# Two residual 64x64 products per batch: the first four units of eight batches in 32x64 TensorE tiles with half-partition stores, the other twelve in 32x128 tiles

## What is computed

```
x = x + einsum('bct,bcd->bdt', x, w0[subjects])      # 8 matrices of 64x64
x = x + einsum('bct,bcd->bdt', x, w1[conditions])    # 200 matrices of 64x64
```

## Time and profile before

| | us |
|---|---|
| median of 3 runs | 92.75 (92.61 to 92.92) |
| the profiled execution | 92.78 |
| its span, first to last instruction | 91.0 |
| outside the span | 1.8 |
| TensorE busy | 78.5 (86%) |
| DVE busy | 61.8 (68%) |
| ACT busy | 58.6 (64%) |
| POOL busy | 23.4 (26%) |
| TensorE's granted clock, mean | 0.989 |

### The profile page before, as it was taken

How to read it: one execution, slowest core, us unless ns; L and a number is a source line. 1 busy time by engine, 2 the same in 40 slices (tenths; PEclk the granted TensorE clock), 3 DMA queues, 4 the chain that set the end, 5 groups by cost and what they waited for, 6 DMA issues and landing times.

```text
span 91.0 us, 2427 instructions
## 1 busy us (share of the span) xinstructions
PE 78.5 (86%) x890; PEld 44.7 (49%) x890; DVE 61.8 (68%) x127; ACT 58.6 (64%) x117; POOL 23.4 (26%) x119
## 2 busy tenths in 40 slices
PE   0499939994999999999999999999999999999200
PEld 0389929983554544364454445445454544444000
DVE  1087008995288888796887878788777888778700
ACT  2899806886276767585777667677666777577500
POOL 3400029999999959300000000000000000000000
PEclk9999999999999999999999999999999999999995
DMA  0999989999999999999999999999999999999993
GB/s 9 334 411 421 461 342 427 412 412 407 411 411 402 412 400 414 409 421 420 418 418 414 423 420 418 416 418 421 423 407 423 418 418 421 421 414 376 414 420 140
DMA packets 9181, 35.93 MB, mean 395 GB/s; under 512 B 721, under 2 KB 850, under 8 KB 9042
## 3 DMA queue, kind: packets, MB, share of 16 engines
q1 hardware_dynamic: 4512, 16.78, 46.3%
q10 hardware_dynamic: 4514, 16.91, 45.8%
q0 software_dynamic: 144, 2.10, 5.4%
HBM read 19.01 MB, written 16.78 MB: 393 GB/s over the span
## 4 chain that ended last, share of the span: by engine, by line
PE 70%; DMA 13%; DVE 9%; issue 1%; DVEq 1%; ACTq 0%; POOLq 0%
PE psum L219 62%; DMA w_rows<-in_L_cond_weights_dram,cond 10%; DVE w L238 7%; PE psum L200 7%; DMA subjects<-in_itok_B_dram 2%; DVEq L69 1%; DVE xy L260 1%; PE psum L180 1%; DVE m_diag L252 1%; ACTq L318 0%; DVE w_rows L313 0%; POOLq L149 0%; DVEq L244 0%
## 5 line engine op out<-in xcount | busy, mean ns | idle before, releaser
L219 PE MATMUL psum<-xy,m_diag 64*128 64x512 f32 x256 | 57.1, 596 | 0.5 <-DVE m_diag L252 0.5
L260 DVE COPY xy<-psum 64x512 f32<-64x512 f32 x64 | 43.7, 683 | 13.2 <-PE psum L219 12.2
L260 ACT COPY xy<-psum 64x512 f32<-64x512 f32 x64 | 37.2, 581 | 19.8 <-PE psum L219 19.0
L219 PEld LDWEIGHTS psum<-xy,m_diag 64*128 64x128 f32 x256 | 24.8, 187 | 27.1 <-issue 25.7
L157 POOL COPY w0b<-w0t 64x64 f32 x112 | 21.6, 235 | 11.0 <-DMA w_rows<-in_L_cond_weights_dram,cond 8.5
L200 PEld LDWEIGHTS psum<-w,w0b 64*32 64x32 f32 x512 | 5.6, 105 | 6.4 <-issue 3.8
L238 ACT COPY w<-psum 64x256 f32<-64x256 f32 x16 | 5.8, 364 | 4.1 <-PE psum L180 3.1
L180 PE MATMUL psum<-ident,w_rows 128*64 128x128 f32 x64 | 7.2, 274 | 1.4 <-DVE w_rows L313 1.4
L252 DVE TENSOR_SCALAR m_diag<-psum,mask 128x256 f32<-128x256 f32 (+1 forms) x18 | 7.3, 449 | 1.1 <-PE psum L200 0.9
L326 ACT COPY w<-w_rows 128x256 f32<-128x256 f32 x18 | 7.3, 405 | 0.9 <-DMA w_rows<-in_L_cond_weights_dram 0.3
L180 PEld LDWEIGHTS psum<-ident,w_rows 128*64 128x64 f32 x64 | 7.0, 152 | 1.6 <-DVE w_rows L313 1.6
(11 more groups left out here) (8 smaller groups left out, 2.3 us busy)
## 6 DMA issues: line engine op xcount, KB each, us to landing
xy<-in_x_dram SPq DMA_DIRECT2D x15, 1024.0 KB, 19.0
out_dram<-xy ACTq DMA_DIRECT2D x15, 1024.0 KB, 11.0
xy<-in_x_dram SPq DMA_DIRECT2D x2, 512.0 KB, 5.9
out_dram<-xy ACTq DMA_DIRECT2D x2, 512.0 KB, 4.3
w_rows<-in_L_cond_weights_dram ACTq DMA_DIRECT2D x1, 128.0 KB, 2.6
cond<-in_itok_B_dram SPq DMA_DIRECT2D x1, 0.5 KB, 2.4
subjects<-in_itok_B_dram ACTq DMA_DIRECT2D x1, 0.5 KB
w_rows<-in_L_cond_weights_dram,cond POOLq DMA_INDIRECT x1, 9.5
```

Of the source, the lines that this page charges most:

```text
L219: last = nc.tensor.matmul(psum[:, 2 * (s % Y_RING) + h, :], m_diag[rows, odd, v % M_RING, j, :], xy[rows, s, j * T:(j + 1) * T], start=j = ...
L260: copy(xy[rows, s, i * T:(i + 1) * T], psum[HALVES[i], 2 * (s % Y_RING) + h, :]).then_inc(done, 1)
```

## The change

The first four units (`SINGLE`) are stored in SBUF as before, in slots. Their stationary operand is now one batch's M alone, `m_single`, with no zeros, in tiles of 32 rows by 64 columns (`apply_single`). What leaves PSUM has one batch's 64 output channels on 64 partitions, four batches side by side, so a unit is stored by two DMAs, each from 64 partitions, in descriptors of one row (2 KB).

The other twelve units lie with four rows of x (8 KB) in a partition and 16 partitions for a batch (`J = 4`), are loaded by one DMA of 1 MB in descriptors of 8 KB, and are multiplied in four tiles of 32 rows by 128 columns with `m_diag` (two batches on the diagonal), four steps `j` for each half of a unit, the second half one step behind the first. Their products are made for two batches at a time with 128 moving columns, of which the mask keeps half. Their stores are as before.

PSUM is handed out as four pairs of banks in a fixed round (`USES`) to products and results. The mask comes from one reduction instead of eight memsets, and w0 is laid out twice, in `w0t_single` and `w0t`. The numbers of x columns, the order of loads, the gather and the filler stay.

```diff
@@ the views, and the rounds of PSUM @@
-    J = 2
+    J = 4
     Q = C // J
...
+    TWOS = 4
+    USES = [("m", 0)]
+    for k in range(BLOCKS):
+        USES += [("y", 4 * k), ("y", 4 * k + 1)]
+        if k + 1 < BLOCKS:
+            USES += [("m", k + 1)]
+        USES += [("y", 4 * k + 2), ("y", 4 * k + 3)]
...
-    x_view = x_dram.rearrange("(s b) (p j) t -> (b p) s (j t)", b=SLOT, j=J)
-    out_view = out_dram.rearrange("(s b) (q i) t -> (b q) s (i t)", b=SLOT, i=J)
+    x_view = x_dram.rearrange("(v b) (p j) t -> (b p) v (j t)", b=UNIT, j=J)
+    single_x_view = x_dram.rearrange("(s r) (p i) t -> (r p) s (i t)", r=PAIRS, i=I)
+    out_view = out_dram.rearrange("(s b) (q i) t -> (b q) s (i t)", b=UNIT // 2, i=I)
+    single_out_view = out_dram.rearrange("(s r) c t -> s c r t", r=PAIRS)
@@ sync @@
-            load(3, 1)
-            for v in range(2, UNITS):
-                load(2 * v, 2)
+            load_slots(3, 1)
+            for v in range(2, SINGLE):
+                load_slots(2 * v, 2)
+            for v in range(SINGLE, UNITS):
+                sp.dma_start(x_of(v), x_view[:, v, :]).then_inc(s_x[v], 16)
@@ tensor: products, the new branch @@
+                    for j in range(J):
                         for r in range(PAIRS):
                             for odd, rows in enumerate(HALVES):
...
+                                last = nc.tensor.matmul(psum[QUARTERS[r], bank("m", k) + odd, j * P:(j + 1) * P],
+                                                        w0b[rows, k, at:at + 2 * Q],
+                                                        w1[rows, n:n + 2, :].rearrange("q b e -> q (b e)"),
+                                                        start=True, stop=True)
@@ tensor: apply @@
-                    for j in range(J):
-                        for h, rows in enumerate(HALVES):
-                            last = nc.tensor.matmul(psum[:, 2 * (s % Y_RING) + h, :],
-                                                    m_diag[rows, odd, v % M_RING, j, :],
-                                                    xy[rows, s, j * T:(j + 1) * T],
-                                                    start=j == 0, stop=j == J - 1)
...
+            def apply(v, half, j):
...
+                for h in range(2):
+                    rows = QUARTERS[2 * half + h]
+                    last = nc.tensor.matmul(psum[:, bank("y", n) + h, :], m_diag[rows, v % M_RING, j, :],
+                                            xy[rows, 2 * v + 2 + j // 2, j % 2 * T:(j % 2 + 1) * T],
+                                            start=j == 0, stop=j == J - 1)
...
+            def apply_single(v, half):
...
+                for i in range(I):
+                    for h in range(2):
+                        rows = QUARTERS[2 * half + h]
+                        for o, columns in enumerate(HALVES):
+                            last = nc.tensor.matmul(psum[columns, bank("y", n) + h, :], m_single[rows, v, o, i, :],
+                                                    xy[rows, 2 * v + 2 + o, i * T:(i + 1) * T],
+                                                    start=i == 0, stop=i == I - 1)
@@ copy_y @@
+            if n < 2 * SINGLE:
+                copy(xy[:, n, i * T:(i + 1) * T], psum[:, bank("y", n) + i, :]).then_inc(done, 2)
+                return
@@ store @@
-            nc.scalar.dma_start(out_view[:, s:s + n, :], xy[:, s:s + n, :]).then_inc(s_out[s // 2], 16)
+            if s < 2 * SINGLE:
+
+                for o, rows in enumerate(HALVES):
+                    nc.scalar.dma_start(single_out_view[s + o], xy[rows, s:s + n, :].rearrange(
+                        "c s (h t) -> c (s h) t", h=2)).then_inc(s_out[s // 2], 16)
+            else:
+                nc.scalar.dma_start(out_view[:, s:s + n, :], xy[:, s:s + n, :]).then_inc(s_out[s // 2], 16)
```

More of the change, by code:

```diff
@@ L43, in bass_cond_residual_kernel @@
     ROWS = S0 * C // P
[L45 to L50, removed]
+    assert ROWS == J
+    M_RING = 4
+    TWOS = 4
[5 more added lines that the diff above has]
+        USES += [("y", 4 * k + 2), ("y", 4 * k + 3)]
     TURN = 4
@@ L191, in products @@
[L191 to L195, removed]
+                if k == 0:
+                    pe.wait_ge(s_w0b_early, BLOCK * UNIT)
+                else:
+                    pe.wait_ge(s_w0b, k * BLOCK * UNIT)
+                wait_for_banks("m", k)
+                if BLOCK * k < SINGLE:
+                    for o in range(2):
+                        for j in range(I):
+                            for r in range(PAIRS):
+                                for odd, rows in enumerate(HALVES):
+                                    at = (o * I + j) * C
+                                    n = PAIRS * o + r
+                                    last = nc.tensor.matmul(psum[QUARTERS[r], bank("m", k) + odd, at:at + C],
+                                                            w0b[rows, k, n * C + j * H:n * C + (j + 1) * H],
+                                                            w1[rows, k * UNIT + n, :], start=True, stop=True)
+                else:
@@ L196, in products @@
                     for j in range(J):
-                        for r in range(SLOT):
+                        for r in range(PAIRS):
                             for odd, rows in enumerate(HALVES):
[L199 to L202, removed]
@@ L227, in _ @@
             products(0)
[L228 to L231, removed]
+            for v in range(UNITS):
+                if v % BLOCK == 1 and v < UNITS - 1:
+                    products(v // BLOCK + 1)
+                wait_for_m(v)
+                pe.wait_ge(s_x[v], 32 if v == 1 else 16)
+                if v < SINGLE:
+                    apply_single(v, 0)
+                    apply_single(v, 1)
+                    continue
+                for j in range(J):
+                    apply(v, 0, j)
+                    if j > 0:
+                        apply(v, 1, j - 1)
+                    elif v > SINGLE:
+                        apply(v - 1, 1, J - 1)
@@ L270, in copies @@
                 copy_w1(eng, copy, w1_done, n)
[L271 to L281, removed]
+            eng.wait_ge(s_mask, 1)
@@ L283, in _ @@
+            for kind, n in USES:
+                if kind == "m":
+                    copy_m(eng, copy, scale, m_done, odd, n)
+                    continue
+                copy_y(eng, copy, y_done, odd, n)
+                if odd and n % 2 == 0 and n > 0:
+                    store(n - 2, 2)
         @block.vector
         def _(dve):
-            for r, rows in enumerate(QUARTERS):
-                for b in range(2):
-                    nc.vector.memset(mask[rows, b:b + 1], 1.0 if b == r % 2 else 0.0).then_inc(s_mask, 1)
@@ L289, in _ @@
             dve.wait_ge(s_ident, 1)
+            nc.vector.tensor_reduce(mask[:, :], ident[:, :].rearrange("q (r b p) -> q b r p", b=2, p=Q),
+                                    axis=mybir.AxisListType.XY, op=ALU.add).then_inc(s_mask, 1)
             dve.wait_ge(s_subjects, 16)
             dve.wait_ge(s_w0_turned, 1)
-            turned = w0_psum.rearrange("q (y j s k) -> q j s k y", y=J, j=J, s=S0)
-            one = ident[0:C, 0:C].rearrange("q (o k y j) -> q j o k y", o=1, y=J, j=J)
             for rows in HALVES:
-                for j in range(J):
+                for i in range(I):
```

158 lines of the change are left out of this document (95 added, 63 removed).

## The result

The changed kernel takes 100.56 us (median of 6 runs), the kernel before 92.68 beside it: a ratio of 1.0817, 95% interval 1.0788 to 1.0847. The forecast was 97.7 us with a range of 92.3 to 99.0. The direction was right; the time lies above the range, and it came about in another way.

What follows compares the result with a forecast made beforehand. The DMA engines bound the kernel: a transfer always waits, so the end is the sum of all packets. 92.78 - 0.77 + 0.54 + 4.8 + 0.5 - 0.2 = 97.65, say 97.7 us, range 92.3 to 99.0.

Steps and rivals of the forecast that it cites:

- part 3: First four units' stores from 64 partitions: 2 KB packets cost 156 instead of 80 ns, +4.8 us behind the loads, +0.5 beside them.
- rival (b): ACT's queue fills with half-store packets, ACT and its copies stand still, TensorE ends near 92, about 99 us; chance 0.10.
- a limit of about 107 packets: How many packets per engine a DMA queue holds, taken from SP's last issue, which took 10.4 us.
- a round of 386 ns: While loads run, a 2 KB store alternates with an 8 KB load on each engine: 306 + 80 ns.
- Part 1: Loads of twelve units: 256 packets become 128 each, 1536 fewer at 8 ns over 16 engines, -0.77 us.
- part 2: Stores of four units: 256 packets become 512 each, plus four more DMAs with their completions, +0.54 us.
- Shares by number: Load and store queues share the DMA engines packet by packet, in equal numbers whatever the packet size.
- rival (c): Queues share engines by bytes, so early stores finish while loads run: 92.4 to 97, about 94.5 us; chance 0.12.
- Part 4: TensorE's chain with the new tiles: 442 ns a step, products taken as 1.1 us, ending at 83.2 instead of 84.9 us.
- rival (d): TensorE's tiles are not packed; 32-row tiles taking turns double 42.5 us, ending over 120 us; chance 0.03.
- The gain of 0.2 us at the dip: DMA share dips at 82 to 85 us; with the queue behind TensorE by then the dip goes, -0.2 us.

Runs made afterwards that it cites:

- SP's stores: The changed kernel with the eight half-partition stores of the first four units issued by SP, behind its loads, instead of ACT: 99.54 us, ratio 1.0686.
- the stores put off: The changed kernel with the first four units' half stores moved behind later units' stores: one unit at a time 102.4 us, all eight in a row 103.69 us.
- the paced one: The changed kernel with 4 KB loads, SP also waiting before each load from unit 9 on until TensorE has done unit v-6: 96.99 us, ratio 1.0429.
- stores of 2 KB: The kernel before with every store cut into two DMAs over all 128 partitions with 2 KB packets: 95.72 us, ratio 1.03.
- the stores in a row: The changed kernel with all eight half-partition stores of the first four units issued in one row behind unit 8's store: 103.69 us, ratio 1.1139.
- The control over 128 partitions: The kernel before with every store cut into two DMAs of half the bytes, each over all 128 partitions: 93.24 us, ratio 1.0035.

## Why the prediction was wrong

**The step that failed is the wait for ACT, which the sum has at nothing.** The forecast has TensorE done near 83 us and puts its loss, 4.8 + 0.5 us, into slow half stores (part 3). That ACT is held by its own queue stands only in rival (b), with a chance of 0.10. The runs showed the reverse: the hold costs 8.2 us of TensorE and 6.6 us of the DMA engines' time, the slow half stores some 0.3 us. Rival (b) had ACT standing from about 36 us, TensorE ending near 92 and a time of about 99. It was 33 to 36 us for the first long issues, a stop of 9.3 us, TensorE's end at 91.3 (the chain's last matmuls begin at 80.63 and last 10.66), and 100.56. The text set it low without an argument, apart from a remark that slow packets would hide it. But everything it needed was in hand: a limit of about 107 packets from SP's own long issue (by the records ACT's held issues of the changed kernel ended at 92 to 95), the 136 packets of four units, and a round of 386 ns, which the same text used for the end of the loads. A forecast that trusts the round must trust the backlog that comes of it. That the time rose, as forecast, is luck: the term that was to raise it hardly came.

**Part 3, +4.8 and +0.5 us**, did not come: by the records the 2 KB packets take 86 ns on the mean and 88 behind the loads, where full rate has 84, so 2048 x 2 / 16 = 0.3 us. The bound was not wrong as such: a mean of 105 to 121 ns over all of them was measured in the runs with SP's stores and with the stores put off, 110 ns in a stretch of the paced one, and a part of the packets lasts 145 to 160 ns in each. What failed is to take a constant upper end for a cost that changes with what else is queued.

**Part 1, -0.77, and part 2, +0.54**, hold: the packet numbers are as counted, and in the records packets of 2, 4, 8 and 16 KB last 84, 159, 310 and 611 ns in the median, a line of 8.5 ns and 37.7 ns for a KB. The 37 ns of the prediction is a slip for 38; its 84 and 312 ns go by 38.

**Shares by number**, against rival (c), hold in three pairs of sizes: 725 to 726, 1173 to 1172, 1011 to 1012. The last load packet of the changed kernel starts at 54.4 us; the loads' end was forecast for 53.2.

**Part 4** holds where ACT does not stop TensorE. Chain of the changed kernel:

```profile
62.94 1.09 PE psum L257 x64
64.03 7.21 PE psum L275 x64
71.24 1.09 PE psum L257 x64
72.33 7.21 PE psum L275 x64
79.54 1.09 PE psum L257 x64
80.63 10.66 PE psum L275 x94
```

The products take 1.09 us (1.1 forecast) and a step 7.21 / 16 = 451 ns (442). Without the hold TensorE ended at 81.3 us with SP's stores and 83.5 with loads of 4 KB; the forecast was 83.2. The gain of 0.2 us at the dip could not appear. The tiles are packed, against rival (d).

Added up by what was measured: 92.78 - 0.77 + 0.54 + 6.6 (DMA engines without work from 68 to 90 us) = 99.2, with 1.2 us of the 100.32 left. By the records the half stores' packets are 2 ns longer, 0.3 us, and the 4 KB stores' last 163.6 in place of 160.1 ns, 0.7 us. The last 0.2 us are not accounted for, and why the 4 KB stores are slower was not asked.

## What to carry to other kernels

When an engine issues DMAs between copies, count the packets that can be outstanding on its queue, how fast they drain beside the other queue's packets, and against what limit: a queue that fills stops the copies, and then the engine that waits for them. Since queues take turns by packet, making one queue's packets larger or the other's smaller moves bandwidth from one to the other, so change the two together. And if a rival follows from the same assumption as the forecast, give it the same chance as that assumption.

## What the runs showed of the hardware that was not expected

- What a queue takes goes by packets far more than by bytes. By the records of the kernel before and the changed one, 80 to 100 were outstanding per DMA engine when an issue held for over 2 us ended, for 2 KB and 4 KB packets on ACT's queue and 4 KB and 8 KB ones on SP's, so four times the bytes at about the same number. It is not one fixed number: with stores of 2 KB, issues of 0.7 us ended with 110 to 113, and SP's loads of 2 KB were held down to 70.
- Transfers from 64 partitions have no rate of their own. The mean of a 2 KB packet over all half stores is 86 ns in the changed kernel, 85 with loads of 4 KB and of 2 KB, 93 with paced loads, 105 with the stores in a row, 117 issued by SP and 121 put off one unit at a time. The control over 128 partitions stays at 160 ns for 4 KB.
- Issuing a DMA from 64 partitions costs 0.6 to 0.7 us, where one with as many packets from 128 takes 0.38 to 0.42, and 1.4 to 2.5 us in the run with the stores in a row, with some 40 packets outstanding. Why stays open.
- The stop costs a little more than itself: the granted clock is 0.88 on the mean from 33 to 50 us and 0.50, the lower level of 1.2 GHz, from 49 to 50 us, behind TensorE's 8.2 us without work. L275 is busy 46.1 us with 617 ns a matmul; the same matmuls take 44.4 us and 600 ns with SP's stores.
